# Moving the normalised rows of two layer norms from VectorE to ScalarE, with an offset computed on GpSimd

## The reference

```
def _layernorm(x, axis=-1, eps=1e-05):
    m = jnp.mean(x, axis=axis, keepdims=True)
    v = jnp.var(x, axis=axis, keepdims=True)
    return (x - m) / jnp.sqrt(v + eps)
...
xn = _layernorm(x, axis=-1)
x = x + _L0_attn_ref(xn, ...) + _L0_ffn_ref(xn, ...)
xn = _layernorm(x, axis=-1)
x = x + _L1_attn_ref(xn, ...) + _L1_ffn_ref(xn, ...)
```

## Time and profile before

| | |
|---|---|
| median of 3 runs | 2019.58 us (2018.63 to 2025.25) |
| profiled execution | 2028.95 us, its span 2026.6 us |
| busy in the span | TensorE 89%, VectorE 68%, ScalarE 57%, GpSimd 22% |
| first normalisation, first statistics to last `keep` | 7.08 to 48.95 us |
| second normalisation, first L228 to last `keep` | 1015.90 to 1071.10 us |

### The profile page before, as it was taken

How to read it: one execution, slowest core, us unless ns; L and a number is a source line. 1 busy time by engine, 2 the same in 40 slices (tenths; PEclk the granted TensorE clock), 3 DMA queues, 4 the chain that set the end, 5 groups by cost and what they waited for, 6 DMA issues and landing times. The chain is left out here.

```text
span 2026.6 us, 33817 instructions
## 1 busy us (share of the span) xinstructions
PE 1802.2 (89%) x10009; PEld 1249.0 (62%) x10090; DVE 1387.4 (68%) x3090; ACT 1158.3 (57%) x2806; POOL 441.1 (22%) x406
## 2 busy tenths in 40 slices
PE   5589999999999798999758988999989898989898
PEld 2456766676676697999624464655556464656555
DVE  5857777877877311222185878888889788888885
ACT  2255566566556221222123338888888878888886
POOL 2032442353244414221110110020202001020101
PEclk9789999999999898999879969999999999999999
DMA  4511221232121484554193672352434333343311
GB/s 167 194 52 63 93 92 62 74 114 72 62 93 63 168 308 165 180 179 166 38 305 111 187 215 60 79 104 73 102 73 100 69 82 85 84 96 85 87 27 32
DMA packets 143790, 226.12 MB, mean 112 GB/s; under 512 B 17725, under 2 KB 110015, under 8 KB 143648
## 3 DMA queue, kind: packets, MB, share of 16 engines
q1 hardware_dynamic: 124464, 179.95, 29.1%
q0 software_dynamic: 19184, 44.45, 8.4%
HBM read 174.26 MB, written 50.99 MB: 111 GB/s over the span
## 5 line engine op out<-in xcount | busy, mean ns | idle before, releaser
L2350 DVE TENSOR_SCALAR att_scores<-att_psS 128x512 f32<-128x512 f32 x512 | 349.2, 682 | 98.3 <-PE att_psS L2180 61.3
L2299 ACT ACTIVATE att_prob<-att_scores,att_shift 128x512 f32<-128x512 f32 x512 | 382.9, 748 | 25.1 <-DVE att_shift L2366 25.1
L2308 ACT COPY att_pT<-att_psT 128x512 f32<-128x512 f32 x512 | 306.1, 599 | 135.8 <-PE att_psT L2188 133.6
L2358 DVE CUSTOM_DVE_ANT_0 att_scores<-att_scores,first_decay 128x512 f32<-128x512 f32 x512 | 348.1, 680 | 0.0
L2188 PEld LDWEIGHTS att_psT<-ident,att_prob 128*128 128x128 f32 x2048 | 245.1, 142 | 159.7 <-issue 100.6
L2188 PE MATMUL att_psT<-ident,att_prob 128*128 128x128 f32 x2048 | 315.4, 277 | 19.5 <-ACT att_pT L2308 15.4
L2202 PE MATMUL att_psO<-att_pT,att_v 128*32 128x512 f32 x1024 | 141.0, 625 | 42.4 <-ACT att_pT L2308 38.0
L2180 PE MATMUL att_psS<-first_ks,first_qs 128*128 128x512 bf16 x431 | 164.7, 383 | 15.5 <-DVE att_scores L2350 12.0
L1576 ACT ACTIVATE ffn_hT<-ffn_psH,ffn_b 128x128 f32<-128x128 f32 x156 | 44.7, 369 | 202.6 <-PE ffn_psH L1532 135.9
L1546 PE MATMUL ffn_psY<-ffn_w,ffn_hT 128*128 x624 | 148.4, 391 | 6.6 <-issue 3.6
L1597 DVE TENSOR_SCALAR ffn_hT<-ffn_psH,ffn_b 128x128 f32<-128x128 f32 x156 | 44.0, 344 | 160.9 <-PE ffn_psH L1532 137.5
(11 more groups left out here) (315 smaller groups left out, 2875.7 us busy)
## 6 DMA issues: line engine op xcount, KB each, us to landing
ffn_w<-in_w SPq DMA_DIRECT2D x39, 1024.0 KB
mamba_am<-a_rows SPq DMA_DIRECT2D x64, 512.0 KB, 3.9
first_qs<-q_parts SPq DMA_DIRECT2D x256, 64.0 KB
first_ks<-k_parts SPq DMA_DIRECT2D x256, 64.0 KB
xn<-xn_all SPq DMA_DIRECT2D x16, 512.0 KB, 5.5
ffn_w<-in_w POOLq DMA_DIRECT2D x8, 1024.0 KB, 6.1
att_w<-in_inter POOLq DMA_DIRECT2D x7, 1024.0 KB, 5.4
att_w<-in_outer POOLq DMA_DIRECT2D x7, 1024.0 KB
```

Source lines behind the costliest of these rows:

```text
L2299: nc.scalar.activation(prob[:, n % NP], scores[:, n % NCL], ACT.Exp, bias=shift[:, h % 2, t:t + 1], accum_out=total[:, octet % 2, t, j, i: ...
L2308: nc.scalar.copy(pT[:, h % HEADS_T, :, t * P:(t + 1) * P], bank_of("turn", n)[:].rearrange("p (k q) -> p k q", k=CPB)).then_inc(pT_ready, 1)
L2350: vec.tensor_scalar(scores[:, n % NCL], psS[n % NS][:], -CLAMP, CLAMP, ALU.max, ALU.min).then_inc(clipped, 1)
L2358: vec.tensor_tensor_reduce(scores[:, n % NCL], scores[:, n % NCL], decay[:, FAR - t * P:FAR - t * P + SEQ], 1.0, -2.0 * CLAMP, ALU.mult, A ...
```

## The change

VectorE no longer writes the normalised rows. ScalarE does, as Identity(scale * x + bias) with scale = rstd and bias = -mean * rstd, both columns of one value for each token. `moments` now scales the sum of the two half means by -0.5 rather than 0.5, so that `mean` holds its negative, and GpSimd multiplies it by rstd into the new `offset`, behind the power and behind a wait for it. `rows_out` stands first in ScalarE's step, `copy` and `copy_products` move one step later in its list: `rows_out(n)`, `copy(n-1)`, `copy_products(n-2)`. The lists of TensorE and SyncE stay as they are. Both normalisations are this one function.

```diff
--- before.py
+++ after.py
@@ -163,6 +163,7 @@
         spread = s.sb("spread", [P, 2, CPB])
         var = s.sb("var", [P, BATCH, CPB])
         rstd = s.sb("rstd", [P, BATCH, CPB])
+        offset = s.sb("offset", [P, BATCH, CPB])
         lT = s.sb("lT", [width, 2, SEQ])
         psT = [[s.psum(f"psT{j}{k}", [P, SEQ]) for k in range(KD)] for j in range(2)]
         psL = [s.psum(f"psL{j}", [P, SEQ]) for j in range(2)]
@@ -176,6 +177,7 @@
         chain = s.sem("chain")
         var_ready = s.sem("var_ready")
         rstd_ready = s.sem("rstd_ready")
+        offset_ready = s.sem("offset_ready")
         xn_ready = s.sem("xn_ready")
         turned = s.sem("turned")
         xT_ready = s.sem("xT_ready")
@@ -237,18 +239,12 @@
                     c.link(v.scalar_tensor_tensor(out=spread[:, q], in0=stats[:, q, :, 2], scalar=D * EPS, in1=stats[:, q, :, 5],
                                                   op0=ALU.add, op1=ALU.add))
                     c.wait()
-                    c.link(v.tensor_scalar(mean[:, b], mean[:, b], 0.5, None, ALU.mult))
+                    c.link(v.tensor_scalar(mean[:, b], mean[:, b], -0.5, None, ALU.mult))
                     c.link(v.scalar_tensor_tensor(out=diff[:, q], in0=diff[:, q], scalar=0.25, in1=diff[:, q], op0=ALU.mult, op1=ALU.mult))
                     c.wait()
                     v.scalar_tensor_tensor(out=var[:, b], in0=spread[:, q], scalar=1.0 / D, in1=diff[:, q],
                                            op0=ALU.mult, op1=ALU.add).then_inc(var_ready, 1)
 
-                def rows_out(b):
-                    dve.wait_ge(rstd_ready, b + 1)
-                    for t in range(CPB):
-                        v.tensor_scalar(xn_all[:, b * CPB + t, :], x[:, b, t], mean[:, b, t:t + 1], rstd[:, b, t:t + 1],
-                                        ALU.subtract, ALU.mult).then_inc(xn_ready, 1)
-
                 def keep(b):
                     dve.wait_ge(turned_back, b + 1)
                     v.tensor_copy(logits[:, b * CPB:(b + 1) * CPB, :], psB[b % 2][:]).then_inc(logits_kept, 1)
@@ -256,8 +252,6 @@
                 for n in range(BATCH + 3):
                     if n < BATCH:
                         moments(n)
-                    if 1 <= n <= BATCH:
-                        rows_out(n - 1)
                     if n >= 3:
                         keep(n - 3)
                 dve.wait_ge(logits_kept, BATCH)
@@ -267,6 +261,8 @@
                 for b in range(BATCH):
                     pool.wait_ge(var_ready, b + 1)
                     nc.gpsimd.tensor_tensor(rstd[:, b], var[:, b], C.half[:, 0:CPB], ALU.pow).then_inc(rstd_ready, 1)
+                    pool.wait_ge(rstd_ready, b + 1)
+                    nc.gpsimd.tensor_tensor(offset[:, b], mean[:, b], rstd[:, b], ALU.mult).then_inc(offset_ready, 1)
 
             @block.tensor
             def _(pe):
@@ -310,6 +306,12 @@
 
             @block.scalar
             def _(act):
+                def rows_out(b):
+                    act.wait_ge(offset_ready, b + 1)
+                    for t in range(CPB):
+                        nc.scalar.activation(xn_all[:, b * CPB + t, :], x[:, b, t], ACT.Identity, bias=offset[:, b, t:t + 1],
+                                             scale=rstd[:, b, t:t + 1]).then_inc(xn_ready, 1)
+
                 def copy(b):
                     act.wait_ge(turned, b + 1)
                     if merge is None and b >= NR:
@@ -327,11 +329,13 @@
                         act.wait_ge(turned_back, b - 1)
                     nc.scalar.copy(lT[:, b % 2], psL[b % 2][0:width, :]).then_inc(lT_ready, 1)
 
-                for n in range(BATCH + 1):
+                for n in range(BATCH + 2):
                     if n < BATCH:
-                        copy(n)
-                    if n:
-                        copy_products(n - 1)
+                        rows_out(n)
+                    if 1 <= n <= BATCH:
+                        copy(n - 1)
+                    if n >= 2:
+                        copy_products(n - 2)
 
 
 
```

## The result

The changed kernel takes 2013.47 us (median of 11 runs, 2007.04 to 2018.62), the kernel before 2027.67 us beside it (11 runs, 2018.63 to 2032.42). The ratio is 0.9937, 95% interval 0.9920 to 0.9954: faster by 9.3 to 16.2 us, 12.8 in the middle. The forecast was 8.9 faster, 2010.7 us, with the range 2008.0 to 2018.0. The profiled execution has a span of 2015.0 us against 2026.6.

A forecast was written before the change was run, and what follows sets the result against it. No engine full: a dependency loop through `keep` and `turn_back` paces both normalisations. Gains of -2.3 and -6.6 sum to -8.9 us, 2020.1 for the profiled execution, shifted by 9.4 to 2010.7; range 2008.0 to 2018.0.

The forecast's parts named there:

- Rival (b): ScalarE's row activations don't overlap, 0.60 each: total -6.1 us, 2013.5; counted within the main case's range, no separate chance.
- Rival (a): GpSimd's new multiply costs what the power costs, 1.04 us: total -3.8 us, 2015.8; chance 0.12.
- The power without L249: GpSimd's power takes 1.04 us once VectorE's row writes are gone, against a mean of 1.23 mostly beside them.
- First normalisation: Stage from 0 to 50 us: period 3.97 against 4.57, end at 46.7 before 48.95, -2.3 us.
- Second normalisation: Stage from 1010 to 1072 us: period 4.83 against 6.18, end at 1064.5 before 1071.1, -6.6 us.
- `keep(0)` at 1034.4 with TensorE slow in the first three batches: Second normalisation: batch 0's `keep` at 1034.4, putting `rows_out(4)` at 1040.0.
- (7) 4.8 later: Second normalisation: `rows_out(7)` at 1054.5, 4.8 us behind `rows_out(6)` at 1049.7.
- (5) follows pass 4 directly: First normalisation: `rows_out(5)` comes straight after ScalarE's pass 4, at 28.60, so (7) is at 36.5.
- Rival (c): TensorE's clock stays low throughout the second normalisation, which gains 0.2: total -2.5 us, 2017.1; chance 0.12.
- Rival (e): Identity and Copy need different tables, so ScalarE reloads twice a pass: slower, 2042 us; chance 0.04.
- Rival (d): Transfers hold the second normalisation, or the gain is lost after the barrier: 0 to -4 us, about 2017; chance 0.09.
- Rival (f): More than 11 us gained, with TensorE at full clock in both normalisations; chance 0.04.

The follow-up runs named there:

- before_keep4: Kernel before with `keep` one batch later in VectorE's list, VectorE still writing the rows; ratio 0.9924 to the kernel before.
- after_keep4: Changed kernel with `keep` one batch later too; ratio 0.9873 to the kernel before.
- second_power_busy: Changed kernel with a second GpSimd power per batch, plus four idle TensorE matmuls around the transposes of batches 3 to 7; ratio 0.9968 to the kernel before.
- first_only: Kernel before with the new order in the first normalisation only; ratio 0.9963 to the kernel before.
- after_warm: Changed kernel with 44 idle matmuls in the first and 64 in the second normalisation before TensorE's first wait; ratio 0.9956 to the kernel before.
- after_warm24: Changed kernel with 24 idle matmuls at the start of the first normalisation alone; ratio 0.9934 to the kernel before.
- second_only: Kernel before with the new order in the second normalisation only; ratio 0.9937 to the kernel before.
- extra_activation: Changed kernel with a fifth, unused 128x256 activation at the head of each batch's rows on ScalarE; ratio 0.9965 to the kernel before.
- second_power: Changed kernel with one more, unused 128x4 power on GpSimd between the multiply and ScalarE's wait; ratio 0.9976 to the kernel before.

## Why the prediction was right, point by point

- *What bounds the stages.* Right: a loop through `keep` and `turn_back`, no full engine. "before_keep4" shows it for the kernel before and "after_keep4" for the changed one, without moving any work.
- *Price of the activations.* Forecast 0.59 for one and 2.00 for four before the copy can follow; measured 0.589, and the copy starts 1.99 behind the first of the four (25.71 to 27.70). Rival (b), no overlap, would be 2.4 and is out.
- *Price of the multiply.* Forecast 0.20; 0.20 measured beside bn_stats or an idle VectorE. Rival (a) is out, and "second_power_busy" shows what it would have cost: its leg grew by 1.1 and the stages by 3.5 and 3.8 us with the clock full from batch 1 on, so the rival's 0.84 would be 2.7 to 2.9 each, 2.5 forecast, and more where the clock falls.
- *The power without L249.* 1.01 in the first normalisation, as the step had it. In the second it took 1.20 to 1.28, and the multiply 0.25 to 0.30, whenever VectorE was in its additions (L230), and 1.01 and 0.20 when it was not (rows at 1044.56 and 1048.49). The forecast took 1.05 there from a power that had started 0.14 before the addition; this step was wrong by up to 0.3 us for every other batch. The rule of the Trainium skill ("SBUF — State Buffer", "Who interferes with whom") that two SBUF inputs on VectorE collide with a GpSimd instruction that reads agrees with these rows in direction; the multiply's loss was 0.1 us, not the 0.42 that was set as its bound.
- *First normalisation.* Forecast -2.3, measured -1.94. The steps alternate at 3.41 and 4.39, as the forecast had it, the pair 7.80 against 7.93; but `rows_out(4)` came at 25.71 rather than 25.13, because the second load landed at 9.90 rather than 9.57, the slow products(0) ended at 20.2 rather than 19.8, and the transposes behind them took 1.40 rather than 1.0. "first_only" with faster first products shows the other end, -3.2.
- *Second normalisation.* Forecast -6.6, measured -8.8, nearer to the forecast's own figure for a full clock, -8.4. Two terms were mis-sized. The step "`keep(0)` at 1034.4 with TensorE slow in the first three batches", 18.5 behind the first addition, was 17.3: products(0) took 2.78 and the next already 1.88. It is 17.3 in "after_warm", "after_warm24" and "second_only" too, where products(0) took 1.88, 2.36 and 3.03: up to there their slowness costs nothing, since ScalarE comes to `copy_products` only at 1029.60, 0.9 behind the end of these products. And "(7) 4.8 later" took the mean period where the passes alternate: the pair measures 3.56 and 6.23, and the last step is of the short kind, 1.3 us less. For the second the step of the first normalisation, "(5) follows pass 4 directly", should have been used here too.
- *Rival (c)*, the low clock, did not happen in the trace of after from 1030 us on, but it is real: "second_only" and "extra_activation" have it in part of their batches. Its price was reckoned with the clock low throughout.
- *Rival (e)*, table loads, is out: one load, at 3.06.
- *Rival (d)*, transfers: "after_keep4" is 4 us shorter in the second normalisation than the changed kernel, so no floor of the transfers held the changed one.
- *The total.* -8.9 forecast; the stages say -10.7, the runs -12.8 with 9.3 to 16.2. The interval holds the stages' sum, but the runs as a whole point to a gain that the two lengths don't show. Set against the trace of before, the lengths of "second_only", "before_keep4", "after_keep4" and "second_power" show 6.2, 9.1, 17.9 and -1.4 us, and their totals 8.2 to 17.3, 10.3 to 20.1, 21.7 to 29.4 and 1.2 to 8.6. In "extra_activation" it is 3.7 against 3.8 to 10.5. The lengths come from one execution of each kernel, and that of the kernel before had the clock low in a part of its second normalisation; whether the rest is chance of that kind or a gain in other stages stays open.
- *Rival (f)*, more than 11 us gained, had a chance of 0.04. The middle of the runs, 12.8, lies in it and the stages' 10.7 just below: the runs don't decide it, and 0.04 looks too little.
- *Luck.* The absolute time, 2010.7 forecast and 2013.47 measured, looks better than it is. The forecast set out from 2019.58 for the kernel before, the median of three runs; beside the changed kernel it took 2027.67. The base was 8.1 us too low and the gain 5.3 too small as a difference of medians, and the two nearly cancel. From 2027.67 the same gain gives 2018.8, above the stated range. What the prediction has to its credit is the loop and its prices, not the closeness of that number.

## What to carry to other kernels

When no engine is full, find the loop before moving work: write down who waits for whom with the batch number of each, and see how many batches the loop spans. Here one line, a drain put one batch later in the hand-written order, gained about as much (ratio 0.9924, against 0.9937 for the change) as moving 20 us of work to another engine, and both together gained 1.3%. Count alternation too: a loop over two passes gives uneven steps, and the end falls on one kind of them.

## What the runs showed of the hardware

- A delay can cost more than the loop asks for, through TensorE's clock. An added wait of 1.1 us per batch cost 6.3 and 5.8 us where the loop asked for 3.3, with some products at 3.4 to 3.6 us instead of 1.90 and a granted clock of 0.83 in a stretch of 10 us; four idle matmuls in each of five batches, 1.3 us of extra work per batch by their rows, made the two stages 2.7 and 2.0 us shorter.
- Idle matmuls of 7.5 us at the start raised the clock, but not for long: transposes of 1.82 us behind them instead of 2.07, granted 1.00 from 10 to 14 us, 0.50 from 14 to 20, and the products 6 us behind them took 3.61 us. After 12.7 us of them, followed without a gap by the transposes, the products took 1.90.
- In the first 20 us of the trace of after the row for the granted clock says 1.00 while the first products take 3.61 us, the duration that goes with a granted 0.50 in "after_warm24": where a trace starts with TensorE idle, its durations tell more of the clock than this row.

```profile
10.00:20.00 10.00, 7.64 (x20) 2.80 (x20) 6.06 (x30) 8.03 (x16) 4.21 (x8) 1.00 0.91 302
```
- A GpSimd multiply of 128x4 in float32 takes 0.20 us, the power of the same shape 1.01, so some 0.8 us of the power goes with the operation and not with starting it.
